# The last layer norm moved from a pass of its own into the steps of the last expert

## What is computed

```
x  = layernorm(x + mamba(x))                 # stage 1 of the kernel
xf = x.reshape(16384, 256)
scores = softmax(xf @ gate_w.T)              # 8 experts
vals, idx = top_k(scores.T, 2048)            # each expert picks 2048 rows
for each expert n, its rows:
    y = layernorm(xf[idx]) * ln_w + ln_b
    h = gelu(y @ fc1[n].T + b1[n])           # 256 -> 1024
    o = (h @ fc2[n].T + b2[n]) * vals        # 1024 -> 256
    xf[idx] += o                             # a row can be picked by several experts
out = layernorm(x + xf)                      # mean and variance over the 256 floats of each row
```

## Time and profile before

| what | value |
|---|---|
| median of 3 runs | 4356.21 us (4354.37 to 4360.1) |
| span of the profiled execution | 4349.7 us |
| median less span | 6.5 us |
| busy share of PE, DVE, ACT, POOL | 81%, 86%, 81%, 80% |
| last PE matmul ends | about 4233.4 us into the span |
| stage 4, first load issued to the end | 4251.1 to 4349.7 us |

### The profile page before, as it was taken

One profiled execution on the slowest core, in us unless ns is written; L12 is line 12 of the kernel. 1 busy time (PEld: TensorE's weight loads), 2 busy tenths in 40 slices (PEclk: granted clock), 3 DMA queues, 4 the chain that ended last, 5 costly groups with the idle time before them and its releaser, 6 DMA issues. The chain is left out here.

```text
span 4349.7 us, 58014 instructions
## 1 busy us (share of the span) xinstructions
PE 3523.5 (81%) x19574; PEld 2466.4 (57%) x19574; DVE 3738.2 (86%) x4784; ACT 3507.4 (81%) x5977; POOL 3499.8 (80%) x1784
## 2 busy tenths in 40 slices
PE   7788888888887878888888887888865599999990
PEld 3455555555555555555555555555554488888880
DVE  5999999999999999999999999999997756666535
ACT  5889999899999999999999999999872355656656
POOL 3899999999899999999999999999883355555533
PEclk9889999999999999999999999999986699999995
DMA  2667767766666777767766667677663233333328
GB/s 88 152 155 171 176 167 166 174 164 167 163 159 162 173 175 171 173 167 165 172 172 161 170 155 165 165 176 171 157 159 52 74 65 61 63 65 63 61 32 312
DMA packets 184230, 626.30 MB, mean 144 GB/s; under 512 B 33905, under 2 KB 99569, under 8 KB 128641
## 3 DMA queue, kind: packets, MB, share of 16 engines
q0 software_dynamic: 74688, 366.52, 42.3%
q1 hardware_dynamic: 104640, 239.32, 16.6%
q10 hardware_dynamic: 4608, 16.78, 1.0%
HBM read 221.47 MB, written 68.68 MB: 67 GB/s over the span
## 5 line engine op out<-in xcount | busy, mean ns | idle before, releaser
L463 POOL TENSOR_TENSOR dbu<-du,bb 128x2048 f32<-128x2048 f32 x511 | 2435.7, 4818 | 100.6 <-DVE h L939 75.8
L939 DVE TENSOR_TENSOR_SCAN h<-da,hlast,dbu 128x512 f32<-128x512 f32 x1536 | 1868.6, 1266 | 80.7 <-POOL dbu L463 55.1
L791 PE MATMUL ht<-ident,h 128*128 128x128 f32 x8192 | 1178.4, 289 | 460.8 <-DVE h L939 179.2
L524 ACT ACTIVATE da<-dl,negA 128x512 f32<-128x512 f32 x2048 | 1413.7, 702 | 122.0 <-DVE h L939 116.5
L791 PEld LDWEIGHTS ht<-ident,h 128*128 128x128 f32 x8192 | 964.6, 147 | 876.0 <-DVE h L939 317.0
L543 ACT ACTIVATE pair<-ht,ct 128x512 f32<-128x512 f32 x896 | 591.7, 688 | 116.6 <-DMA acc<-pair 60.5
L939 DVE TENSOR_TENSOR_SCAN h<-da,dbu 128x512 f32<-128x512 f32 x512 | 593.0, 1207 | 43.2 <-POOL dbu L463 22.7
L715 PE MATMUL spare<-xin,win 128*128 128x512 f32 x1024 | 495.8, 615 | 11.8 <-DMA xin<-in_xt 7.4
L724 PE MATMUL spare<-xh,conv 128*128 128x512 f32 x1024 | 463.7, 596 | 0.8 <-ACT xh L555 0.8
L1569 ACT ACTIVATE hraw<-f,b 128x512 f32<-128x512 f32 x256 | 176.3, 689 | 265.2 <-PE f L1640 249.1
L1496 POOL DMA_INDIRECT sums<-ot,idx x128 | 204.6, 1598 | 211.9 <-DVE ot L1824 182.7
(11 more groups left out here) (224 smaller groups left out, 5607.0 us busy)
## 6 DMA issues: line engine op xcount, KB each, us to landing
acc<-pair POOLq DMA_DIRECT2D x222, 1024.0 KB, 7.3
bb<-b_rows SPq DMA_DIRECT2D x128, 1024.0 KB, 6.5
acc<-acc POOLq DMA_DIRECT2D x64, 1024.0 KB, 8.0
dl<-du POOLq DMA_DIRECT2D x62, 512.0 KB, 5.9
xin<-in_xt SPq DMA_DIRECT2D x32, 512.0 KB, 5.0
x_scores<-xres SPq DMA_DIRECT2D x32, 512.0 KB, 4.5
sums<-xres SPq DMA_DIRECT2D x32, 512.0 KB, 6.2
rows<-sums SPq DMA_DIRECT2D x32, 512.0 KB, 6.0
```

The costliest lines, as they stand in the source:

```text
L463: pool.tensor_tensor(dbu[n % 2][:], du[q][:], bb[part % 2][:, m:m + 1, :].to_broadcast([P, DT, CH]), ALU.mult).then_inc(dbu_done, 1)
L524: act.activation(da[DA_SLOT[m]][:], dl[q][:, dt, :], ACT.Exp, scale=negA[:, dt, n:n + 1]).then_inc(exp_done, 1)
L791: last = te.transpose(ht[HT_SLOT[m]][:, dt * P:(dt + 1) * P], h[n % 2][:, dt, b * P:(b + 1) * P], ident[:])
L939: dve.tensor_tensor_scan(h[n % 2][:, dt, :], da[DA_SLOT[n * DT + dt]][:], dbu[n % 2][:, dt, :], start, ALU.mult, ALU.add).then_inc(scan_do ...
```

## The change

Stage 4 goes. Its work is done in 16 tiles of 1024 rows (8 rows a partition, 1 MB) inside stage 3, from the first step of the last expert on. The rows that the last expert picks are handled apart ("late" rows): their values in `sums` are gathered into `xg[t]` once that group's input rows are used up, the expert's result is added to them in SBUF, they are normed there, and they are written straight to `out` by index, after the 16 plain tiles have been stored. So nothing of the last expert is added to `sums`, and the plain tiles hold wrong values for its rows until these are overwritten. Tiles 1, 3, 5, 7, 9, 11, 14 are normed by POOL (8 `tensor_scalar` each), the others by ACT (8 `activation` each): two in step 1, one in step 2, six after the gelus of step 3. The five 8 KB buffers are memory that the last expert doesn't use any more; all stores are issued by SP. `UNITS` is the order in which DVE makes statistics and POOL the powers.

```diff
-        onehot = [a.sb(f"onehot{i}", [P, G // 2, P, 2], BF16) for i in range(OH)]
+        onehots = a.sb("onehots", [P, OH, G // 2, P, 2], BF16)
+        onehot = [onehots[:, i] for i in range(OH)]
...
+        LAST = E - 1
+        R = 8
+        PAIRS = n_tok // (P * R)
+        UNITS = [("late", 0), ("rows", 0), ("rows", 1), ("rows", 2), ("late", 1), ("rows", 3), ("rows", 4), ("rows", 5),
+                 ("late", 2), ("rows", 6), ("rows", 7), ("rows", 8), ("late", 3)] + [("rows", k) for k in range(9, PAIRS)]
+        BY_POOL = (1, 3, 5, 7, 9, 11, 14)
+        BY_ACT = {1: (0, 2), 2: (4,), 3: tuple(k for k in range(5, PAIRS) if k not in BY_POOL)}
+        ACT_PAIRS = [k for t in (1, 2, 3) for k in BY_ACT[t]]
+        row_view = d["acc"].rearrange("(n p r) f -> n p (r f)", p=P, r=R)
+        out_view = d["out"].rearrange("(n p r) f -> n p (r f)", p=P, r=R)
+        row_bufs = [d["wide"], wraw[:], rhs[:].bitcast(F32).rearrange("p s g a t two -> p (s g a t two)")] + [
+            onehots[:, 2 * i:2 * i + 2].bitcast(F32).rearrange("p o g t two -> p (o g t two)") for i in range(2)]
+        NBUF = len(row_bufs)
+        late = [x[:, :, 0:256] for x in xg]
...
+                def final_rows():
+                    def load(k):
+                        sp.dma_start(row_bufs[k % NBUF], row_view[k]).then_inc(rows_in[k % NBUF], 16)
+                    for k in range(NG):
+                        sp.wait_ge(added[k], 64 * LAST)
+                    sp.sem_inc(sp_passed3, 1)
+                    sp.wait_ge(w_rest, 2 * E)
+                    sp.sem_inc(sp_passed3, 1)
+                    sp.wait_ge(oh_used, E * SL)
+                    for k in range(NBUF):
+                        load(k)
+                    for k in range(PAIRS):
+                        s, v = rows_normed(k)
+                        sp.wait_ge(s, v)
+                        sp.dma_start(out_view[k], row_bufs[k % NBUF]).then_inc(rows_out[k % NBUF], 16)
+                        j = k - 1
+                        if j >= 0 and j + NBUF < PAIRS:
+                            sp.wait_ge(rows_out[j % NBUF], 16 * (j // NBUF + 1))
+                            load(j + NBUF)
                 def step(e, t, p, following, later, ahead):
                     if not following:
+                        if t == 0:
+                            final_rows()
                         return
                     if t == 0:
...
+                def late_rows(some):
+                    for t in some:
+                        pool.wait_ge(xn_ok, LAST * NG + t + 1)
+                        pool.sem_inc(pool_passed, 1)
+                        for b in range(4):
+                            pool.indirect_dma_start(
+                                out=late[t][:, b, :], out_offset=None, in_=d["acc"],
+                                in_offset=bass.IndirectOffsetOnAxis(
+                                    ap=idx[LAST % 2][:, 4 * t + b:4 * t + b + 1], axis=0)).then_inc(late_in[t], 16)
+                def final_rstd(kind, i):
+                    x, n = unit(kind, i), R if kind == "rows" else 4
+                    pool.wait_ge(var4, x + 1)
+                    pool.tensor_tensor(rstd4[:, x, 0:n], ve4[:, x, 0:n], half[:, 0:n], ALU.pow).then_inc(rstd4_ok, 1)
+                    pool.wait_ge(rstd4_ok, x + 1)
+                    pool.tensor_tensor(shift4[:, x, 0:n], nmean4[:, x, 0:n], rstd4[:, x, 0:n], ALU.mult
+                                       ).then_inc(shift4_ok, 1)
+                def final_norm(k):
+                    x, tile = unit("rows", k), row_tile(k)
+                    pool.wait_ge(shift4_ok, x + 1)
+                    for r in range(R):
+                        last = pool.tensor_scalar(tile[:, r, :], tile[:, r, :], rstd4[:, x, r:r + 1],
+                                                  shift4[:, x, r:r + 1], ALU.mult, ALU.add)
+                    last.then_inc(rows_pool, 1)
+                def last_step(t):
+                    if t == 0:
+                        scatter(LAST - 1, NG - 1, 1 - LAST % 2)
+                        rstd_and_shift(LAST * NG + 2)
+                        gather(LAST, 3, LAST % 2)
+                        for k in range(NG):
+                            pool.wait_ge(added[k], 64 * LAST)
+                        late_rows((0, 1, 2))
+                        final_rstd("late", 0)
+                        final_rstd("rows", 0)
+                        rstd_and_shift(LAST * NG + 3)
+                    elif t == 1:
+                        for kind, i in UNITS[2:5]:
+                            final_rstd(kind, i)
+                            if kind == "rows" and i in BY_POOL:
+                                final_norm(i)
+                        late_rows((3,))
+                        for kind, i in UNITS[5:]:
+                            final_rstd(kind, i)
+                            if kind == "rows" and i in BY_POOL:
+                                final_norm(i)
                 def step(e, t, p, following, later, ahead):
+                    if e == LAST:
+                        last_step(t)
+                        return
...
                 run(prologue, step)
-                scatter(E - 1, NG - 1, 1)
-                for k in range(NG):
-                    pool.wait_ge(added[k], 64 * E)
+                for b in range(NBUF):
+                    pool.wait_ge(rows_out[b], 16 * ((PAIRS - 1 - b) // NBUF + 1))
+                pool.sem_inc(pool_passed, 1)
+                for t in range(NG):
+                    pool.wait_ge(late_normed, t + 1)
+                    for b in range(4):
+                        pool.indirect_dma_start(
+                            out=d["out"], out_offset=bass.IndirectOffsetOnAxis(
+                                ap=idx[LAST % 2][:, 4 * t + b:4 * t + b + 1], axis=0),
+                            in_=late[t][:, b, :], in_offset=None).then_inc(late_out, 16)
+                pool.wait_ge(late_out, 16 * 4 * NG)
 
...
                     if ahead >= 2:
                         normalise(grp + 2, (t + 2) % NG)
+                    if e == LAST:
+                        for k in BY_ACT.get(t, ()):
+                            final_norm(k)
+                def final_norm(k):
+                    x, tile = unit("rows", k), row_tile(k)
+                    act.wait_ge(shift4_ok, x + 1)
+                    for r in range(R):
+                        last = act.activation(tile[:, r, :], tile[:, r, :], ACT.Identity, bias=shift4[:, x, r:r + 1],
+                                              scale=rstd4[:, x, r:r + 1])
+                    last.then_inc(rows_act, 1)
 
...
+                def final_stats(kind, i, some):
+                    x = unit(kind, i)
+                    n = R if kind == "rows" else 4
+                    tile = row_tile(i) if kind == "rows" else late[i]
+                    if some[0] == 0:
+                        if kind == "rows":
+                            dve.wait_ge(rows_in[i % NBUF], 16 * (i // NBUF + 1))
+                        else:
+                            dve.wait_ge(merged, i + 1)
+                    for r in some:
+                        last = dve.bn_stats(stats4[:, x % 2, r, :], tile[:, r, :])
+                    if some[-1] < n - 1:
+                        return
+                    last.then_inc(st4, 1)
+                    dve.wait_ge(st4, 2 * x + 1)
+                    for r in range(n):
+                        last = dve.bn_aggr(mv4[:, x, r, :], stats4[:, x % 2, r, :])
+                    last.then_inc(st4, 1)
+                    dve.wait_ge(st4, 2 * x + 2)
+                    dve.tensor_scalar(nmean4[:, x, 0:n], mv4[:, x, 0:n, 0], -1.0, None, ALU.mult)
+                    dve.tensor_scalar(ve4[:, x, 0:n], mv4[:, x, 0:n, 1], LN_EPS / 4, None, ALU.add).then_inc(var4, 1)
+                def late_norm(t):
+                    x = unit("late", t)
+                    dve.wait_ge(shift4_ok, x + 1)
+                    for b in range(4):
+                        last = dve.tensor_scalar(late[t][:, b, :], late[t][:, b, :], rstd4[:, x, b:b + 1],
+                                                 shift4[:, x, b:b + 1], ALU.mult, ALU.add)
+                    last.then_inc(late_normed, 1)
+                def last_step(t):
+                    grp, e = LAST * NG + t, LAST
+                    inner = 3 * t - 2
+                    for m in range(FM):
+                        rest_of_hidden(dve, m, grp)
+                        if m == 5 and t < 2:
+                            row_stats(grp + 2, e, t + 2)
+                            variance(grp + 2)
+                        if m % 2 == 1 and t > 0:
+                            final_stats("rows", inner, range(m - 1, m + 1))
+                    if t < 3:
+                        rest_of_input(grp + 1)
+                    dve.tensor_scalar(score[:, t, :], xg[t][:, :, 256 + e], 0.5, None, ALU.mult).then_inc(scored, 1)
+                    if t > 0:
```

(35 more changed lines are left out.)

106 lines of the change are left out of this document (23 added, 83 removed).

## The result

The changed kernel takes 4335.41 us (median of 4 runs, 4328.62 to 4336.49) against 4357.76 us before (4 runs, 4354.37 to 4360.1): ratio 0.9947, 95% interval 0.9935 to 0.9959. The forecast was 4323.5 in 4311 to 4342, faster: the sign and the range held, the likeliest value was 12 us too low. In a later comparison (e11) the same kernel took 4345.0 us (4337.95 to 4345.78, 5 runs), ratio 0.9964 [0.9951, 0.9978]: still faster, but outside the range of the forecast.

What follows compares the result with a forecast made beforehand. PE bounds the last expert's steps, memory traffic and ACT together stage 4. Steps, tail and scatters put the span's end near 4317 against 4349.7 (-33); plus 6.5 gives 4323.5 us, range 4311 to 4342.

Steps and rivals of the forecast that it cites:

- Stage 1 and 2: Before the last expert's overlap: everything up to the bias at 4162.0 stays as it was.
- PE's end: End of step 3: PE's last result at 4245.4 instead of 4233.4, a price of 12 us.
- Step 0: Group 28: merge waits for late gather until 4168, hidden_rest comes late, ACT and PE lose 6.9 us, PE's clock falls.
- Step 1: Group 29: ACT waits for tile 2's shift, norms last until 4197.9, next gelu 3.5 us later; delay then 10.4.
- The tail up to tile 15's store: After PE's last result at 4245.4: DVE's seven remaining tiles, then loads decide; tile 15's store down at 4294.
- The scatters: Very end: POOL issues 16 plain scatters, 0.3 + 15 x 1.25 + 3 = 22 us.
- Rival (1): Final scatters: a plain scatter costs what the adding one does, +9.6 us, 4333; chance 0.17.
- The end of the stage: After the scatters: span ends near 4317, with the meeting of engines at stage 3's end counted as removed.
- (2): Norms by POOL: a row costs 1.1 us, holding ACT in step 1 and the tail, +10 us, 4334; chance 0.10.
- (4): POOL becomes the bound: slower than before from 1.7 us a norm row, 4374 us at 2.16; chance 0.04.
- Rival (3): Step 0: loads hold the late gathers up, landing in 10 to 12 us, +7 us, 4331; chance 0.11.
- Rival (5): Steps' stalls cost nothing, gathers land in 2.8 us: 4317; held within the forecast's own spread, chance 0.55 together.

Runs made afterwards that it cites:

- e11: The changed kernel as it is, measured and profiled a second time: 4345.0 us, ratio 0.9964 against the kernel before.
- e8: Changed kernel with late rows gathered first, tile 0's statistics early, loads spread, sixth buffer, ACT norms a step later, tile 15 normed by DVE: 4337.4 us.
- e12: Changed kernel with at most four indirect transfers in a row, six buffers, early tile 0 statistics, tile 15 by DVE: 4324.57 us, ratio 0.9927.
- e1: Changed kernel without the 16 final scatters of late rows: end 985.8 us after the start of stage 2, tail 23.3 us shorter.
- e9: Changed kernel with POOL's run of 16 indirect transfers split into 8, then 4, 4 and 4: 2 us above e11.
- e10: Changed kernel without the 12 late gathers of tiles 0 to 2, leaving 4 indirect transfers in a row: 4327.98 us.
- e3: Changed kernel with tile 0's late gather ahead of group 31's gather and tile 0's statistics ahead of the bias: PE ends 10 us later.
- e5: Changed kernel with two 1 MB loads issued first, three more once late gathers have landed: shortest run 4332.12 us.

## Why the prediction was right, and where it was off

The profiled span came out at 4334.7 instead of 4317, 17.7 us more. By the steps of the prediction:

- **Stage 1 and 2**: 6.6 us. Stage 2 began later than in the profile before; no kernel changes it.
- **PE's end**: forecast 12 us later than before, measured 15.7: 3.7 us. Step 0 was right (merge 4174.94 against 4168 + the 6.6 = 4174.6; gelu's stall 7.60 against 6.9; the clock fell, mean 0.83). Step 1's wait of ACT for tile 2's shift came (2.67 us before the norm at 4202.29). Too small in it was POOL's power on 8 columns, which I priced as one on 4; and `hidden_rest` 0 of group 31 made ACT late by 2.4 us instead of 1.6.
- **The tail up to tile 15's store**: 49.7 us against 48.6. DVE was faster than I had (3.57 us a tile instead of 3.9: statistics of tile 9 begin at 4260.39, of tile 10 at 4263.96), the loads slower: DVE waited 0.96, 3.66 and 1.3 us for them.
- **The scatters**: 22.4 us against 22. Rival (1) is out: a plain scatter takes 0.97 + 0.30 us.
- **The end of the stage**: 6.9 us from the last landing to the end of the span, where I had 1. This is the step that failed, by 5.9 us. I read 5.13 us of meeting of engines at the end of stage 3 as removed, and did not put it back at the new end; in the last stage of the kernel before POOL issued no transfer, and its DRAIN took 0.99 us, beside other work.

The first error is chance, the last is mine: POOL's DRAIN had to be looked up at the end of stage 3 in the kernel before, where it stands with its duration:

```profile
L1414 POOLq DRAIN  x1: 5127/5127/5127, 4245.7 to 4245.7; - x1
```

```profile
L1852 POOLq DRAIN  x1: 990/990/990, 4339.4 to 4339.4; - x1
```

Against it stood 4.7 us in my favour: only 1.8 us lie around a span (4336.49 less 4334.7), not the 6.5 that I took as median less span; so the profiled execution before, at 4349.7, was a short one. So 17.7 - 4.7 = 13.0 us are the profiled run's miss of 4323.5. That the result lay in the range is in part luck: the same kernel took 4345.0 in the later comparison, 3 us outside it, with an effect that stands nowhere in my sum.

Of the prices, in groups of POOL by line and shape (count, busy us, mean ns), the norm by POOL and the two widths of power in the changed kernel:

```profile
L1590 POOL TENSOR_TENSOR rstd<-ve,half 128x8 f32<-128x8 f32 x16 | 27.8, 1738 | 21.4 <-DVE ve L1938 21.3
...
L1651 POOL DMA_INDIRECT out<-xg,idx x16 | 15.5, 972 | 13.4 <-DMA out<-scores_and_rows 8.8 <-issue 4.6
...
L1600 POOL TENSOR_SCALAR wraw<-wraw,rstd,shift 128x256 f32<-128x256 f32 x16 | 8.8, 568 | 0.2
...
L1590 POOL TENSOR_TENSOR rstd<-ve,half 128x4 f32<-128x4 f32 x4 | 4.1, 1021 | 10.1 <-DVE ve L1938 10.1
```

A row by POOL costs 0.57 us (0.5 in the prediction; rivals (2) and (4) are out). Tile 3's norm, beside `hidden_rest`, took 6.23 us instead of 4.5, the 1 or 2 us that the Trainium skill ("SBUF — State Buffer", Who interferes with whom) had made me expect for that tile alone. I had overlooked tile 5, beside DVE's merge, which has two inputs as well: 5.15 us, two of its rows at 0.96. The Trainium skill's 1.8 cycles an element ("GPSIMD Engine Reference", Elementwise — side-by-side cycle accounting) had given 0.38 us a row: here the measurement decides, at 0.57. The power takes 1.74 us on average for 8 columns (1.64 alone or beside DVE's statistics) against 1.02 for 4; I had 1.04 for both. Rival (3), gathers held up by the loads, was off: the last late gather of tile 0, issued at 4170.11, was there at 4174.91, 4.8 us later, where I had 4 to 4.5. Rival (5) is out as the stalls came.

What no rival held is the late event. In the profiled run of the change it did not happen, which is why my account of that run adds up; in e11 PE's last result came 5 us later (930.2 against 925.0). I had priced the 12 gathers as POOL's time and as traffic, and both prices were right. The third effect, on an engine that has no part in the transfers, could not be read in the trace before: no run of POOL's transfers beside PE is longer than four there, and all events of PE are on time.

## What to carry to other kernels

When a stage is moved under another, read the end of every block in the trace before, DRAIN rows too, and charge them wherever the new end is: here 6.4 us. Where TensorE is the bound, try GpSimd's gathers in runs of four or so with something between (it took 4337.4 to 4324.6 us from e8 to e12), and look for "remote" waits when an engine gets its events late. And before you explain 10 us between two profiles, align them at a point behind the unchanged part, see whether that part shows the same effect in small, and profile the same program twice.

## What the runs showed of the hardware that I had not expected

- TensorE's semaphore events reached DVE and ACT 1.7 to 14.6 us later than the matmuls' recorded ends let expect, in groups 28 and 29 of ten profiles (e1 to e9, e11), while GpSimd issued 8 to 16 gathers in a row (1.25 us each) or up to 3 us after. Beside runs of four (e10, e12, and the unchanged groups of all twelve) they were at most 0.8 us late, once 1.8 (e9), with the DMA engines full (1.01, 417 GB/s) or not. Two profiles, one of them with 16 in a row, have no late event at all.
- In six of them two events of the first layer came 0.08 to 0.1 us apart, though the matmuls of one take 1.4 us (e3 at 4183.60 and 4183.68, e5 at 4172.64 and 4172.74), as if they were held and let go together.
- GpSimd's DRAIN at the end of a block in which it had issued indirect transfers: 5.13 us (before, e1), 5.46 (e10), 6.44 (the change), 6.60 (e12), all after the last landing. Where it had issued none, the DRAIN lasted as long as the engine's last operation: 4.48 us around one of 4.38 in stage 2, 0.99 around a power of 1.01 in stage 4 of the kernel before.
- A GpSimd `pow` of 128x8 takes 1.64 us alone or beside DVE's statistics, of 128x4 1.01; beside `hidden_rest` or `yt_rest`, which have two inputs, 128x8 took 1.95 to 2.08 (all in the changed kernel). An operation of a few columns is not free, nor one of fixed price.
